# Postnorm layers and a codebook FFN on one core: the layers' slots, the layers' end and the last tile in another order, and one gathered group fewer

## What is computed

```python
h = x @ Win.T + bin                               # 2048 x 64
for layer in range(4):
    y = silu(layernorm(h))
    y = sconv(y)                                  # a complex linear recurrence along the tokens
    h = h + y * sc_lin
    y = silu(layernorm(h) @ W1.T + b1)            # 64 -> 256
    h = h + y @ W2.T + b2                         # 256 -> 64
x1 = _layernorm(x + layernorm(h) @ Wout.T + bout)
Wg, Wu = codebook[idx_gate], codebook[idx_up]     # 1376 x 512 each, in pieces of 8
Wd = codebook[idx_down]                           # 512 x 1376
out = _layernorm(x1 + (silu(x1 @ Wg.T) * (x1 @ Wu.T)) @ Wd.T)
```

## Time and profile before

| | |
|---|---|
| median of 3 runs (lowest, highest) | 1266.31 us (1262.34, 1267.86) |
| the profiled execution: its time, its span | 1264.5 us, 1262.5 us |
| PE, DVE, POOL, ACT busy | 94%, 80%, 74%, 21% |
| indirect DMAs on POOL: for Wd, for units | 688, 192 |
| quads | 304 |
| set-up and first quads, layers, layers' end, main stage, last tile (about) | 0 to 94, 94 to 236, 236 to 291, 291 to 1200, 1200 to 1262.5 us |

### The profile page before, as it was taken

One profiled execution on the slowest core, in us unless ns is written; L12 is line 12 of the kernel. 1 busy time (PEld: TensorE's weight loads), 2 busy tenths in 40 slices (PEclk: granted clock), 3 DMA queues, 4 the chain that ended last, 5 costly groups with the idle time before them and its releaser, 6 DMA issues.

```text
span 1262.5 us, 16835 instructions
## 1 busy us (share of the span) xinstructions
PE 1188.8 (94%) x5595; PEld 839.3 (66%) x5595; DVE 1011.6 (80%) x2194; ACT 261.7 (21%) x395; POOL 929.9 (74%) x895
## 2 busy tenths in 40 slices
PE   6857998889999999999999999999999999999998
PEld 4533444346777777777777777777777777778876
DVE  3998898878997778888777888778888778888845
ACT  2325777772000000000000000000000000000024
POOL 6777777777777777777777777777777777777710
PEclk8968999989999999999999999999999999999999
DMA  9331211102433223433223433333433333334303
GB/s 202 64 68 37 45 37 39 27 4 53 105 92 87 65 71 80 95 82 92 65 69 79 89 85 81 65 70 86 93 85 87 67 70 79 94 72 88 60 2 133
DMA packets 96971, 93.57 MB, mean 74 GB/s; under 512 B 53549, under 2 KB 57909, under 8 KB 96886
## 3 DMA queue, kind: packets, MB, share of 16 engines
q1 hardware_dynamic: 64692, 83.86, 23.0%
q0 software_dynamic: 28160, 3.66, 8.5%
q10 hardware_dynamic: 4034, 4.98, 1.4%
HBM read 87.53 MB, written 4.90 MB: 73 GB/s over the span
## 4 chain that ended last, share of the span: by engine, by line
POOL 73%; issue 21%; PE 4%; DMA 1%; DVE 0%; ACT 0%; POOLq 0%; SPq 0%; DVEq 0%
POOL stage_down L400 57%; POOL stage_up L389 16%; PE bank L652 2%; PE cand L652 2%; DMA work<-in_L_ffn_idx_up 0%; DMA stage_down<-in_L_ffn_codebook,idx_down 0%; ACT x L505 0%; POOLq L160 0%; DVE chosen L1229 0%; DVE x L1033 0%; PE bank L924 0%; SPq L315 0%; DVE idx_low L1091 0%; DVE idx_low L1092 0%; DVE shift L1239 0%
## 5 line engine op out<-in xcount | busy, mean ns | idle before, releaser
L400 POOL DMA_INDIRECT stage_down<-in_L_ffn_codebook,idx_down x688 | 722.3, 1050 | 209.7 <-issue 209.1
L652 PE MATMUL cand<-one_hot,book 128*128 128x512 f32 (+1 forms) x2432 | 622.7, 398 | 19.0 <-DVE one_hot L1057 19.0
L1057 DVE TENSOR_SCALAR one_hot<-bc,low_of 128x512 fp32r<-128x512 uint16 (+1 forms) x1216 | 512.8, 482 | 99.0 <-PE cand L652 97.3
L652 PEld LDWEIGHTS cand<-one_hot,book 128*128 128x128 f32 x2432 | 449.7, 189 | 187.2 <-DVE one_hot L1057 51.8
L389 POOL DMA_INDIRECT stage_up<-in_L_ffn_codebook,idx_up x192 | 205.6, 1071 | 63.8 <-issue 58.2
L652 PE MATMUL bank<-x1t_hi,w 128*128 128x512 f32 (+1 forms) x704 | 239.1, 396 | 0.0
L1075 DVE SCALAR_TENSOR_TENSOR chosen<-bc,high_of,cand 128x512 f32<-128x512 uint16 (+1 forms) x304 | 220.2, 724 | 21.1 <-PE bank L652 17.9
L652 PEld LDWEIGHTS bank<-x1t_hi,w 128*128 128x128 f32 (+1 forms) x704 | 130.3, 185 | 31.4 <-issue 2.1
L652 PE MATMUL bank<-x1t_lo,w 128*128 128x512 f32 (+1 forms) x352 | 137.7, 391 | 0.0
L598 ACT ACTIVATE prod<-bank 128x512 f32<-128x512 f32 (+1 forms) x44 | 26.3, 599 | 389.4 <-PE bank L652 389.4
L605 ACT ACTIVATE act_hi<-prod 128x512 fp32r<-128x512 f32 x40 | 25.3, 633 | 342.5 <-DVE prod L1033 342.5
(11 more groups left out here) (181 smaller groups left out, 751.8 us busy)
## 6 DMA issues: line engine op xcount, KB each, us to landing
bc<-index_parts SPq DMA_DIRECT2D x272, 256.0 KB, 3.3
stage_down<-in_L_ffn_codebook,idx_down POOLq DMA_INDIRECT x688, 2.7
bc<-index_parts_rest SPq DMA_DIRECT2D x32, 192.0 KB, 3.1
x<-in_L_attn_x ACTq DMA_DIRECT2D x4, 1024.0 KB, 9.8
out_x<-x SPq DMA_DIRECT2D x16, 256.0 KB, 2.0
stage_up<-in_L_ffn_codebook,idx_up POOLq DMA_INDIRECT x192
index_parts<-parts_t SPq DMA_DIRECT2D x20, 32.0 KB, 2.0
w_in<-in_L_attn_W ACTq DMA_DIRECT2D x2, 256.0 KB
```

The source lines that it names most:

```text
L400: pool.indirect_dma_start(stage_down[k % RING][:, q, j * CS:(j + 1) * CS], None, a["L0_ffn_codebook"], bass.IndirectOffsetOnAxis(ap=idx_do ...
L652: return pe.matmul(dst, lhs, rhs, start=start, stop=stop)
L1057: done = v.tensor_scalar(one_hot[quad % 2][:, q, 0:nw], bc[quad % BCS][:, 0:nw], low_of[:, q:q + 1], None, ALU.is_equal)
```

## The change

- In a slot, PE does `mixed(t-1)` last (behind `spread(t-2)`, ahead of a second quad) and no longer first; `d` becomes two buffers; DVE does `add_mixed(t-1)` behind `choose` of the slot's first quad and no longer first, and `add_back` ahead of `norm2`; ACT does `silus(t-2)` ahead of `square2(t-1)`. Semaphore counts follow.
- At the layers' end, ACT does both last pairs of Silus in a row and the roots of items 16, 14, 15 and of tile 0 ahead of them; `spread(15)` comes ahead of `back(14)`, `variance1(17)` behind it; `back(15)` moves to step 2, and the roots and squares of the last chunks move by a step.
- Unit 10 (the sixth tile's gate) is no longer in `POOLED`: 11 gathered units, 176 indirect DMAs, 308 quads. `UP_AFTER` places the later groups anew.
- In the last tile, `turn_down(10)` comes one chunk later, and the `down` products run two chunks behind `hidden`, not one.

```diff
-    BOTH = (0, 5)
+    BOTH = (0,)
-    UP_AFTER = (0, 0, 4, 7, 13, 17, 20, 24, 25, 26, 30, 33)
+    UP_AFTER = (0, 0, 4, 7, 13, 17, 20, 24, 27, 31, 34)
...
+        d = [work[:, n, :] for n in (6, 13)]
...
@@ ACT, slot
+                if t >= 2:
+                    silus(t - 2)
                 if t:
                     square2(t - 1)
-                if t >= 2:
-                    silus(t - 2)
                 square1(t + 1)
...
@@ ACT, layers' end
             square2(ITEMS - 1)
+            root2(ITEMS - 1)
+            tile_root(0)
             silus(ITEMS - 2)
+            silus(ITEMS - 1)
             square1(ITEMS + 1)
-            root1(ITEMS + 1)
-            root2(ITEMS - 1)
...
@@ PE
             def mixed(i):
                 pe.wait_ge(s["damped"], i + 1)
-                if i >= 3:
-                    pe.wait_ge(s["h_made"], i - 2)
-                mm(bank[0][:, :], mix[:, i // NC, :], d).then_inc(s["mixed"], 1)
+                if i:
+                    pe.wait_ge(s["h_mid"], i)
+                if i >= 2:
+                    pe.wait_ge(s["h_made"], min(ITEMS - NC + 1, i - 1))
+                mm(bank[0][:, :], mix[:, i // NC, :], d[i % 2]).then_inc(s["mixed"], 1)
...
-                if t:
-                    mixed(t - 1)
                 variance1(t)
...
                 if t >= 2:
                     spread(t - 2)
+                if t:
+                    mixed(t - 1)
...
@@ PE, layers' end
             back(ITEMS - 3)
+            variance2(ITEMS - 1)
             project(0)
             spread(ITEMS - 2)
             project(1)
+            spread(ITEMS - 1)
+            back(ITEMS - 2)
             variance1(ITEMS + 1)
-            variance2(ITEMS - 1)
-            back(ITEMS - 2)
...
@@ PE, last tile
-            for c in range(NC + 1):
+            for c in range(NC + 2):
                 if c < NC:
                     hidden(FULL, REST, c, 0, 1)
-                if c == 0:
+                if c == 1:
                     turn_down(FULL, REST)
-                else:
-                    for t in range((c - 1) * TPC, c * TPC):
+                if c >= 2:
+                    for t in range((c - 2) * TPC, (c - 1) * TPC):
...
@@ DVE, slot
-                if t:
-                    add_mixed(t - 1)
                 one_hots(quads[0] + 1)
...
+                if t >= 3:
+                    add_back(t - 3)
                 if t >= 2:
                     norm2(t - 2)
-                if t >= 3:
-                    add_back(t - 3)
...
+                if t >= 2:
+                    v.wait_ge(s["mixed"], t - 1)
+                tt(d[t % 2], g, tab[:, l, :], ALU.mult).then_inc(s["damped"], 1)
+                choose(quads[0])
                 if t:
-                    v.wait_ge(s["mixed"], t)
-                tt(d, g, tab[:, l, :], ALU.mult).then_inc(s["damped"], 1)
-                choose(quads[0])
+                    add_mixed(t - 1)
```

More of the change, by code:

```diff
@@ L226, in build @@
             tab = at("tab", [P, L, C])
-            work = at("work", [P, 13, C])
+            work = at("work", [P, 14, C])
             h = at("h", [P, T])
@@ L235, in build @@
             centre = at("centre", [P, P])
-        sq1, rs1, xn, y, u, g, d = (work[:, n, :] for n in range(7))
+        sq1, rs1, xn, y, u, g = (work[:, n, :] for n in range(6))
+        d = [work[:, n, :] for n in (6, 13)]
         sq2 = [work[:, 7 + b, :] for b in range(2)]
@@ L561, in _, with tile_root @@
                     kept += 1
+            def tile_root(n):
+                act.wait_ge(s["aggregated"], n + 1)
+                root(rstd[:, n:n + 1], mv[:, n, 1:2]).then_inc(s["rstd_made"], 1)
             root1(ITEMS)
@@ L566, in _ @@
             square2(ITEMS - 1)
+            root2(ITEMS - 1)
+            tile_root(0)
             silus(ITEMS - 2)
+            silus(ITEMS - 1)
             square1(ITEMS + 1)
-            root1(ITEMS + 1)
-            root2(ITEMS - 1)
-            for n in range(NT + 2):
+            for n in range(1, NT + 2):
                 if n == 2:
-                    silus(ITEMS - 1)
                     square1(ITEMS + 2)
+                if n == 3:
+                    root1(ITEMS + 2)
                 if n == 4:
-                    root1(ITEMS + 2)
-                if n == 5:
                     square1(ITEMS + 3)
-                if n == 7:
+                if n == 6:
                     root1(ITEMS + 3)
@@ L584, in _ @@
                     normalize(n - 1, n, "x1_made")
+                if n == 1:
+                    root1(ITEMS + 1)
                 if n < NT:
-                    act.wait_ge(s["aggregated"], n + 1)
-                    root(rstd[:, n:n + 1], mv[:, n, 1:2]).then_inc(s["rstd_made"], 1)
+                    tile_root(n)
             def down_hi(k, n):
@@ L866, in variance2 @@
                     pe.wait_ge(s["state_kept"], t // NC * (NC - 1) + t % NC)
-                if i:
+                if i == ITEMS - 1:
+                    pe.wait_ge(s["rs2_made"], i)
+                elif i:
                     pe.wait_ge(s["ff_made"], i)
@@ L872, in back @@
                 pe.wait_ge(s["ff_made"], i + 1)
-                pe.wait_ge(s["h_mid"], min(ITEMS, i + 3))
+                pe.wait_ge(s["h_mid"], i + 2 if i < ITEMS - 3 else ITEMS)
                 if i:
@@ L881, in spread @@
                 pe.wait_ge(s["normed2"], i + 1)
[L882 to L883 removed]
+                if i == ITEMS - 1:
+                    pe.wait_ge(s["ff_made"], i)
+                pe.wait_ge(s["rs1_made"], min(ITEMS + 1, i + 3))
+                pe.wait_ge(s["rs2_made"], i + 1 if i < ITEMS - 2 else ITEMS)
                 for k in range(FK):
@@ L958, in _ @@
             project(1)
+            spread(ITEMS - 1)
+            back(ITEMS - 2)
             variance1(ITEMS + 1)
-            variance2(ITEMS - 1)
-            back(ITEMS - 2)
             for n in range(1, NT + 1):
+                if n == 2:
+                    back(ITEMS - 1)
                 if n == 3:
                     variance1(ITEMS + 2)
-                    back(ITEMS - 1)
-                if n == 6:
+                if n == 5:
                     variance1(ITEMS + 3)
@@ L969, in _ @@
                     project(n + 1)
-                if n == 1:
-                    spread(ITEMS - 1)
                 if n in AHEAD_STEPS:
@@ L1319, in _ @@
             add_mixed(ITEMS - 1)
+            norm2(ITEMS - 2)
             norm_last(0)
-            norm2(ITEMS - 2)
             add_back(ITEMS - 3)
@@ L1401, in _ @@
                     product_lo(FULL, REST, c)
-                if c == 0:
+                if c == 1:
                     down_lo(FULL, REST)
+                if c >= 3:
+                    make_shift((c - 3) * TPC, TPC, NT + c - 2)
                 if c >= 2:
-                    make_shift((c - 2) * TPC, TPC, NT + c - 1)
-                if c:
-                    for t in range((c - 1) * TPC, c * TPC):
+                    for t in range((c - 2) * TPC, (c - 1) * TPC):
                         add_down(last_pair, t, (bank[2][:, :], cand[0][:, :], cand[1][:, :], cand[2][:, :]))
```

15 lines of the change are left out of this document (7 added, 8 removed).

## The result

The changed kernel takes 1312.17 us (median of 4 runs, 1311.07 to 1314.22), the kernel before 1266.82 on the same chip: a ratio of 1.0367, interval 1.0339 to 1.0395. Slower, as forecast, but by 45 us and not by 24, and above the top of the range (1307). Its profiled execution took 1312.09 us with a span of 1310.3.

The account below looks back on a forecast made before the run. It took PE's work to bound the main stage and a loop of waits across engines the layers; 8.9 + 0 + 5 + 2 + 8.5 - 0.3 = +24.1 on 1264.5 gave 1288.6, forecast 1290 us, range 1274 to 1307.

Parts of the forecast that it names:

- Part 1: Layers' slots: `add_mixed` enters the loop, 9.97 us a slot; +8.9 us over eleven slots, 0 for the first four.
- Part 2: PE's clock in the slots: a wait of about 2.8 us lowers it, 0 to 2.2 us a slot; +5 us taken.
- Part 3: Layers' end from scan 15: regrouped Silus gain nothing, 0 at full clock, up to +6, down to -4; +2 us taken.
- both step alike: Layers' end: once tile 4 is added, at S + 28.3, the kernels before and after run the same.
- Part 4: Main stage, unit 10 looked up whole: 4 quads more less a gathered group's transposes, on PE and DVE, +8.5 us.
- main-stage phases of another length for the same count of quads: Main stage: a sign, listed last, that would show the forecast wrong.
- up to 4 parts later: POOL's gathers: later groups stand up to this much later in the order, and have as much time to spare.
- Part 5: Last tile: the 0.34 us wait for the gather goes, -0.3 us; 0 to +1 for the later outputs.
- chain (d): Rival: POOL sets the kernel's end, so its 21.8 us come off, 1245 us; 2%.
- (a): Rival, layers' slots: taking `mixed` out opens the loop, slots fall to DVE's 8.3 us, 1260 us; 7%.
- (b): Rival, layers: the slot stays as before and only the quads are paid, 1274.5, or 1272 or 1277 us; 14%.
- (c): Rival, layers: the low clock in every slot, +24 for 5 and +6 for 2, 1313 us; 10%.

Follow-up runs that it names:

- e11_tiles_filler: `e10b_end_filler` plus a dummy 128x256 product on PE ahead of the turn of each of tiles 2 to 7: 1291.43 us, ratio 1.0193.
- e4_filler: The changed kernel with one or two dummy 128x512 products on PE ahead of `variance1` in slots from 3 on: 1301.17 us, ratio 1.0265.
- e10b_end_filler: `e4_filler` plus four dummy products at the layers' end, two ahead of `spread(15)` and two ahead of `variance1(17)`: 1293.96 us, ratio 1.0215.
- the padding: The changed kernel with one unused row more allocated in `idx_up`, 64 bytes per partition, no instruction changed: 1305.59 us, ratio 1.0325.
- e6c_open: The changed kernel with ACT's `square2(t-1)` moved behind `square1(t+1)` and the table load: 1307.12 us, ratio 1.0326.

## Why the prediction was wrong, and where it was right

**Part 1, the slot: right, with one term short.** The loop was named rightly and costs 9.92 us for 9.97. With PE kept busy (`e11_tiles_filler`), six one-quad slots take 59.5 us, but the other five 54.9, where the prediction had 50.6: the step that failed is "so the slots with two quads [...] come out at about the same 10.0". The three two-quad slots took 10.77 to 11.87 us, since DVE's second `choose` and one-hots stand ahead of the product with the root. One took 10.53, where a unit's `w` is subtracted ahead of `add_mixed`, as foreseen. The last took 10.40: ACT copies a looked-up unit (`keep_picked`) between the load and the roots, which the loop had no link for.

```profile
231.47 1.28 ACT L559 ACT_TABLE_LOAD   x1
...
232.77 0.60 ACT L460 ACTIVATE w<-bank 128x512 fp32r<-128x512 f32 x1
...
233.26 1.26 ACT L428 ACTIVATE work<-bank,eps 128x512 f32<-128x512 f32 x2
```

The term is 12.9, not 8.9. The first four slots, priced at 38.7, took 39.9 with PE kept busy.

**Part 2, the clock: right mechanism, mis-sized.** "I take half the slots at 1 us, +5 us". Measured, 124.09 - 114.43 = 9.7 us in the eleven slots: a slot in which the clock falls costs up to 2.5 us (12.45 for 9.92), above the bound of 2.2: the root came 0.86 us late for 0.8, and the rest, 1.67 for 1.4, came through `back`, which took 3.78 us where 3.46 was the price. The clock fell in about half the slots, as taken, but at twice the price. That PE's wait would be 2.8 us was right (2.85), except where `add_up` stands in it. Some 1.4 us of the +3.0 ahead of scan 4, where the prediction had no clock term, is the clock's as well (scan 0 to 4: 41.3 us, 39.9 in `e11_tiles_filler`, 38.9 before). The rule cited there (the Trainium skill, "TensorE: Matmul & The Clock Gate", Part 1), that activity is what releases the throttle, agrees with `e4_filler`: more work, 11 us less.

**Part 3, the layers' end: the largest miss.** The chain was right to 0.3 us (S + 22.8 and S + 28.1 in `e10b_end_filler`). The step that failed is "I take +2" out of a bound of +6 for the clock: it took 8.9, for it fell not only around `spread(15)` but again while the tiles were turned, where the prediction had "both step alike". The bound counted five late products and not the tiles behind them. The end has three table loads on ACT where it had five, and at full clock gained nothing from it; the loads took 1.28 us each, and the root or Silu came 0.01 to 0.02 us behind them, so the price of the Trainium skill ("ScalarE: Activation LUTs", What ACT_TABLE_LOAD costs) with a drain of about 1380 ns is not what the trace shows.

**Part 4, the unit looked up: right, with a term missing.** Tile 4's phase costs 8.5 us more with the padding, as priced (7.7 by the whole stretch). What was missing is the 5.1 us of the tiles' place in SBUF. No row of before could show it; the sign to look for was named last in the prediction ("main-stage phases of another length for the same count of quads"). One reading was off: no later group stands "up to 4 parts later". By unit, unit 11's group comes ahead of part 20 and no longer 24, unit 13's ahead of 24 for 25, and those of units 15, 17 and 19 one part later. As no gather was waited for, nothing came of it.

**Part 5: right.** -0.5 for -0.3, and -0.6 alone. POOL had its room: no wait of PE for a gather, and chain (d) fell with it.

**The rivals.** (a), the open loop, did not come, and `e6c_open` shows that opening the loop through ACT's squares would not have brought it: the slot stays at 9.77 us. (b), the slot of before, is out by the quick slots of 9.92 us. (c), the low clock in every slot, at 1313, is nearest to the number, but only some half of it is its mechanism: of the 23.7 us of span beyond the forecast's 24.1 the clock made 13.0 (4.7 more in the slots, 6.9 more at the end, 1.4 ahead of scan 4), the slots at the full clock 4.0, the main stage 4.3, the first slots 1.6 and the end's order 1.0, less 0.2 at the tail. The clock fell in some slots and not in every one, and the rest made up for it by chance. Its 10% was too low all the same: the two clock terms were priced as separate accidents, though both have one cause, PE emptied of work between its waits.

## What to carry to other kernels

When a reordering makes PE wait longer in a loop, price the clock with the loop: take the rows at the lower level for every product until one runs at its old length again, and follow them into the stages behind. A dummy product into a bank that is about to be overwritten is a cheap test (and here a partial cure) of whether lost time is the clock's. And when a buffer ahead of others in SBUF changes size, compare the mean ns of unchanged products before blaming the order of the work.

## What the runs showed of the hardware that I had not expected

The same products of 128x512 took 394 or 395 ns instead of 391 or 392 when tiles that they read lay 64 bytes earlier in SBUF, 5.1 us of a 1300 us kernel; other distances were not tried. The granted clock fell to 0.50 behind a wait of 2.85 us in one order and behind two of 0.83 and 0.82 us in another, and in one and the same kernel a wait of 1.85 us once cost it and once did not; what of a slot's pattern lets it fall stays open. And 32 added products took 20.7 us off a kernel in which PE was already busy 94% of the span.
